# Block 0's TensorE products in pieces of 32 array columns, and the self weighing over 128 rows

## What is computed

```python
def _L0_xcond_ref(x, noise_emb, context, src_mask, ctx_mask, ...):
    NL, D, H, DFF = (6, 128, 16, 512)
    HD = D // H
    ...
    for i in range(NL):
        xn = _adaln(x, noise_emb, n1_w[i], n1_b[i])
        qkv = xn @ qkv_w[i].T
        q, k, v = jnp.split(qkv, 3, axis=-1)
        ...                                # rope on q and k
        a = _attn(q, k, v, src_mask).reshape(B, L, D) @ so_w[i].T
        x = x + a
        xn = _adaln(x, noise_emb, n2_w[i], n2_b[i])
        q = _rope((xn @ cq_w[i].T).reshape(B, L, H, HD))
        k = _rope((context @ ck_w[i].T).reshape(B, LC, H, HD))
        v = (context @ cv_w[i].T).reshape(B, LC, H, HD)
        a = _attn(q, k, v, ctx_mask).reshape(B, L, D) @ co_w[i].T
        x = x + a
        xn = _adaln(x, noise_emb, n3_w[i], n3_b[i])
        h = jax.nn.gelu(xn @ f1_w[i].T + f1_b[i], approximate=False)
        x = x + (h @ f2_w[i].T + f2_b[i])
    return x
```

## Time and profile before

| | |
|---|---|
| median of 3 runs | 6555.9 us (6546.36 to 6572.31) |
| the profiled execution's own time | 6555.0 us |
| its span, first to last instruction | 6553.2 us |
| mean granted TensorE clock | 0.953 of full speed |
| block 0, first weighing's transposes to last | 224.8 to 3390 us of the span |
| matmuls (and as many weight loads) in the span | 56229 |

### The profile page before, as it was taken

How to read it: one execution, slowest core, us unless ns; L and a number is a source line. 1 busy time by engine, 2 the same in 40 slices (tenths; PEclk the granted TensorE clock), 3 DMA queues, 4 the chain that set the end, 5 groups by cost and what they waited for, 6 DMA issues and landing times.

```text
span 6553.2 us, 141305 instructions
## 1 busy us (share of the span) xinstructions
PE 6048.2 (92%) x56229; PEld 4426.8 (68%) x56229; DVE 3934.0 (60%) x8724; ACT 3319.4 (51%) x6401; POOL 2241.2 (34%) x2180
## 2 busy tenths in 40 slices
PE   5899899998999989999989999999789999989998
PEld 4666576665766657666653777777557777756983
DVE  3777777777777777777765334444544444444553
ACT  1565666656566565666653334444333333333763
POOL 4555555555555555555520000000001111146440
PEclk8899999999999999999989899999889999999998
DMA  2665656756566565675750010000100000021000
GB/s 58 103 112 86 102 95 100 107 94 105 92 101 110 91 102 96 102 110 90 112 97 1 18 37 31 29 29 29 26 15 10 15 15 11 15 86 33 1 2 22
DMA packets 396488, 407.90 MB, mean 62 GB/s; under 512 B 125575, under 2 KB 372946, under 8 KB 393786
## 3 DMA queue, kind: packets, MB, share of 16 engines
q1 hardware_dynamic: 395834, 398.85, 34.4%
HBM read 158.00 MB, written 0.46 MB: 24 GB/s over the span
## 4 chain that ended last, share of the span: by engine, by line
PE 69%; DVE 9%; POOL 8%; issue 6%; ACT 4%; DMA 2%; POOLq 1%; SPq 1%; DVEq 0%; ACTq 0%
PE psum L2224 10%; PE psum L2191 9%; PE psum L1554 6%; PE psum L1542 6%; PE psum L1528 6%; PE psum L2235 4%; PE psum L1568 4%; PE psum L1576 3%; POOL slot_context L3410 3%; PE psum L1674 2%; DVE row_max L1898 2%; PE psum L434 2%; PE psum L420 2%; PE psum L1683 1%; POOLq L3417 1%
## 5 line engine op out<-in xcount | busy, mean ns | idle before, releaser
L1898 DVE TENSOR_REDUCE row_max<-psum 112x1 f32<-112x500 f32 x2304 | 1442.0, 668 | 274.1 <-PE psum L1542 269.4
L2019 ACT ACTIVATE weights<-psum 125x448 f32<-125x448 f32 x2304 | 1152.5, 544 | 734.0 <-PE psum L1528 718.6
L1528 PEld LDWEIGHTS psum<-query_stack,key_stack 121*125 121x125 bf16 x9216 | 838.4, 140 | 360.9 <-issue 163.9
L1542 PE MATMUL psum<-key_stack,query_stack 97*112 97x500 bf16 x2304 | 904.8, 393 | 103.3 <-DVE row_max L1898 80.3
L1528 PE MATMUL psum<-query_stack,key_stack 121*125 121x112 bf16 x9216 | 921.2, 223 | 72.8 <-ACT weights L2019 65.0
L2775 POOL TENSOR_TENSOR l_ctx_v<-l_ctx_v,l_ctx_w 125x512 f32<-125x512 f32 x48 | 60.8, 1268 | 2186.2 <-DVE l_ctx_v L2769 2186.2
L2224 PE MATMUL psum<-l_ctx_v,l_turned 125*128 125x128 f32 x5376 | 713.7, 281 | 15.9 <-ACT l_turned L2260 12.2
L2302 DVE TENSOR_REDUCE l_stat<-psum 128x1 f32<-128x1500 f32 (+1 forms) x224 | 391.6, 1748 | 543.6 <-PE psum L2191 543.6
L2224 PEld LDWEIGHTS psum<-l_ctx_v,l_turned 125*128 125x128 f32 x5376 | 643.1, 191 | 49.4 <-ACT l_turned L2260 39.7
L1554 PE MATMUL psum<-weights,values 125*17 125x112 f32 x18432 | 674.9, 265 | 0.2 <-ACT weights L2019 0.2
L1554 PEld LDWEIGHTS psum<-weights,values 125*17 125x17 f32 x18432 | 378.0, 97 | 260.6 <-ACT weights L2019 138.7
(11 more groups left out here) (537 smaller groups left out, 10262.5 us busy)
## 6 DMA issues: line engine op xcount, KB each, us to landing
key_stack<-key_parts SPq DMA_DIRECT2D x1728, 125.0 KB, 4.5
ctx_t<-in_ctxT SPq DMA_DIRECT2D x96, 750.0 KB
l_ctx_v<-in_ctxV SPq DMA_DIRECT2D x32, 750.0 KB
query_stack<-query_parts SPq DMA_DIRECT2D x576, 28.0 KB, 3.6
l_ctx_t<-in_ctxT SPq DMA_DIRECT2D x16, 750.0 KB
slot_context<-in_ctxV SPq DMA_DIRECT2D x16, 750.0 KB
key_stack<-ctx_mask_rows SPq DMA_DIRECT2D x576, 3.9 KB
sm_w<-in_sm_w SPq DMA_DIRECT2D x3, 2048.0 KB
```

The lines of the kernel that those rows point to most:

```text
L1528: mm = e.matmul(self.k.psum[0:KN, h, (p % 4) * QC:(p % 4 + 1) * QC], ks[:, p, kt * KN:(kt + 1) * KN], q[:, p * QC:(p + 1) * QC])
L1542: e.matmul(self.k.psum[0:QC, 2 + n % 2, 0:500], q[0:ROWS_MAX, p * QC:(p + 1) * QC], ks[0:ROWS_MAX, p, c * 500:(c + 1) * 500]).then_inc(sel ...
L1898: e.tensor_reduce(self.largest[:, i % PAIRS, i // PAIRS:i // PAIRS + 1], k.psum[0:QC, 2 + i % 2, 0:500], AX.X, ALU.max, negate=True).then_ ...
L2019: e.activation(half(self.p[kt % 2], h), self.k.psum[0:KN, h, 0:HALF], ACT.Exp).then_inc(self.exped.sem, 1)
```

## The change

A helper, `quarters`, does a product in pieces of up to 32 stationary columns, each to its own 32 output partitions, with the same moving operand. All the products of block 0 that had a wider stationary operand go through it: scores, maxima, keys, values, projections, norms, MLP, self scores and their mask. The weighings had 17 columns already. The transposes of fp32 data (1584, 1591, 1683, 1703, 1710) stay whole. The bf16 transpose takes only the 25 columns that are used. The self weighing now runs over 128 rows: `self_pt` and `self_v` have 128 partitions, the rows of `self_v` past the 56 tokens are zero, and the copies into `self_pt` take all partitions.

```diff
+def quarters(e, out, lhsT, rhs, **kw):
+
+    m = lhsT.shape[1]
+    for lo in range(0, m, 32):
+        hi = min(lo + 32, m)
+        mm = e.matmul(out[lo:hi], lhsT[:, lo:hi], rhs, **kw)
+    return mm
...
-            self.spt = [sb(f"self_pt{i}", [S, H * S])[:, :] for i in range(2)]
-            self.sv = sb("self_v", [S, BH, PAIRS, 17])
+            self.spt = [sb(f"self_pt{i}", [128, H * S])[:, :] for i in range(2)]
+            self.sv = sb("self_v", [128, BH, PAIRS, 17])
...
-            mm = e.matmul(self.k.psum[0:KN, h, (p % 4) * QC:(p % 4 + 1) * QC], ks[:, p, kt * KN:(kt + 1) * KN],
+            mm = quarters(e, self.k.psum[0:KN, h, (p % 4) * QC:(p % 4 + 1) * QC], ks[:, p, kt * KN:(kt + 1) * KN],
                           q[:, p * QC:(p + 1) * QC])
...
-        e.matmul(self.k.psum[0:QC, 2 + n % 2, 0:500], q[0:ROWS_MAX, p * QC:(p + 1) * QC],
+        quarters(e, self.k.psum[0:QC, 2 + n % 2, 0:500], q[0:ROWS_MAX, p * QC:(p + 1) * QC],
                  ks[0:ROWS_MAX, p, c * 500:(c + 1) * 500]).then_inc(self.max_scored.sem, 1)
...
-            e.transpose(side.bank(*key)[:, 0:QC // 2].bitcast(BF16), self.m_part,
+            e.transpose(side.bank(*key)[0:1 + 3 * PAIRS, 0:QC // 2].bitcast(BF16), self.m_part[:, 0:1 + 3 * PAIRS],
                         k.ident_b[0:QC, 0:QC]).then_inc(side.filled, 1)
...
                 for r in range(R):
-                    mm = e.matmul(bk[:, r * S:(r + 1) * S], self.qd[:, i % 2, r * 128:(r + 1) * 128],
+                    mm = quarters(e, bk[:, r * S:(r + 1) * S], self.qd[:, i % 2, r * 128:(r + 1) * 128],
                                   of_batch(self.k_rot, b), start=False, stop=True, skip_group_check=True)
...
-                e.tensor_copy(self.spt[i % 2][:, BANK:T], side.bank(*key)[0:S, 0:T - BANK]).then_inc(side.emptied(*key), 1)
+                e.tensor_copy(self.spt[i % 2][:, BANK:T], side.bank(*key)[:, 0:T - BANK]).then_inc(side.emptied(*key), 1)
...
+        e.memset(self.sv[:, :, :, :], 0.0)
```

More of the change, by code:

```diff
@@ L1599, in fixed_tensor @@
             e.wait_ge(side.emptied(*key), side.before(*key))
-            e.matmul(side.bank(*key)[:, 0:QC], self.co, self.att).then_inc(side.filled, 1)
+            quarters(e, side.bank(*key)[:, 0:QC], self.co, self.att).then_inc(side.filled, 1)
         if 0 <= s + 1 < NS and kt == 10:
@@ L1620, in phase_tensor @@
                 e.wait_ge(side.emptied(*key), side.before(*key))
-                e.matmul(side.bank(*key)[:, 0:HALF], k.mean_w, half(k.z, c)).then_inc(side.filled, 1)
+                quarters(e, side.bank(*key)[:, 0:HALF], k.mean_w, half(k.z, c)).then_inc(side.filled, 1)
             if t == at + 2:
@@ L1632, in phase_tensor @@
             e.wait_ge(side.emptied(*key), side.before(*key))
-            e.matmul(side.bank(*key)[:, 0:HALF], self.wm[:, f, :], half(k.xn, c)).then_inc(side.filled, 1)
+            quarters(e, side.bank(*key)[:, 0:HALF], self.wm[:, f, :], half(k.xn, c)).then_inc(side.filled, 1)
         if mlp is not None and t == T_DOWN:
@@ L1639, in phase_tensor @@
             for f in range(4):
-                mm = e.matmul(side.bank(*key)[:, 0:HALF], self.wm[:, 4 + f, :], self.hidden(f), start=f == 0, stop=f == 3)
+                mm = quarters(e, side.bank(*key)[:, 0:HALF], self.wm[:, 4 + f, :], self.hidden(f), start=f == 0, stop=f == 3)
             mm.then_inc(side.filled, 1)
@@ L1649, in phase_tensor @@
             e.wait_ge(side.emptied(*key), side.before(*key))
-            e.matmul(side.bank(*key)[:, 0:HALF], self.wa[:, (0, 1, 4)[n], :], half(k.xn, c)).then_inc(side.filled, 1)
+            quarters(e, side.bank(*key)[:, 0:HALF], self.wa[:, (0, 1, 4)[n], :], half(k.xn, c)).then_inc(side.filled, 1)
         if t - T_SV in range(2):
@@ L1715, in phase_tensor @@
                 e.wait_ge(side.emptied(*key), side.before(*key))
-                e.matmul(side.bank(*key)[:, 0:QC], self.wa[:, 3, :], self.satt).then_inc(side.filled, 1)
+                quarters(e, side.bank(*key)[:, 0:QC], self.wa[:, 3, :], self.satt).then_inc(side.filled, 1)
     def tensor(self, e):
@@ L1877, in vector @@
         e.memset(self.m_part[:, 0:1], 1.0)
-        e.memset(self.sv[:, :, :, 0:1], 1.0)
+        e.memset(self.sv[0:S, :, :, 0:1], 1.0)
         e.memset(k.psum[:, 5, :], 0.0)
```

14 lines of the change are left out of this document (7 added, 7 removed).

## The result

| | before | after |
|---|---|---|
| time, us (median, lowest to highest, runs) | 6555.1 (6546.4 to 6572.3, 4) | 6700.1 (6685.4 to 6706.7, 4) |
| span of the profiled execution, us | 6553.2 | 6697.6 |
| block 0, first transposes to last, us | 225 to 3391 | 211 to 3534 |

The ratio is 1.0209, with a 95% interval of 1.0184 to 1.0234: the change costs 2.1%, 145 us. The forecast was 6310 us, with a range up to 6542. Block 0 takes 157 us more (3323 against 3166) and starts 14 us earlier; what comes behind it takes the same time in both. So the loss is where the change is.

The account below looks back on a forecast made before the run. TensorE's order of work was taken to set the pace in block 0. Savings of 225 + 65 + 77 = 367 us, two thirds kept (245), took 6555 to 6310 us; whole range 6188 to 6542, the forecast's own 6190 to 6430.

Parts of the forecast that it names:

- Step 1: Block 0, changes of TensorE's tiling shape: 833 fewer pairs at 0.27 us each, 225 us saved.
- Step 2: Score products in block 0: with overlapping loads each of 9216 takes 50 ns, 7 less, 65 us saved.
- Step 3: Self scores in block 0: 14 passes of 107 ns take 50 ns each in pieces, 77 us saved.
- Step 4: Maxima, keys, values, MLP, projections: stream longer than load, so four pieces abreast cost what one whole product does, 0.
- B: Scores and maxima: bf16 pieces don't stream four abreast at full rate; about 7050 us at factor 2, chance 0.08.
- C: The 2304 score halves: each start takes 25 ns whatever its length; 6735 us, chance 0.07.
- D: Weight loads of the score pieces: they go one after another, costing 212 us; 6542 us, chance 0.08.
- Step 5: Issue of 49500 more pairs of matmul and load, nearly all in block 0: taken as 0, bound 92 us.
- Rival E: Block 0: TensorE's instructions arrive too late, some tens of us up to some hundreds; chance 0.04 on the slow side.
- Step 6: The rest: no wait added, self weighing's copies as long as before, one memset more; no cost in us given.
- what is late next: Block 0's slots: VectorE and chains through other engines limit the gain; two thirds of 367 us kept, 245 us.
- rival A: Block 0: VectorE and the DMA queues take most of the saving; with a third kept 6433 us, chance 0.13.

Follow-up runs that it names:

- light transfers: Changed kernel with block 0's key copies cut to 50 of 500 columns and context transfers to 125 columns in later slots, engines' work the same: 6401.9 us.

## Why the prediction was wrong

**Step 1, shape changes: right.** The losses of 0.10 on entering and 0.12 on leaving are gone where pieces stand on either side, and stay where a transpose follows (0.50 us). 0.27 for a pair fits the sums above. Around the value products it was a little more: the weighing and the values behind it took 1.48 us before (1508.67 to 1510.15) and take 1.26 now, which with the 0.10 in front of the weighing is 0.32, and undoing it there cost 0.29.

**Step 2, scores: right.** 16 pieces in 0.20 us are 50 ns a product. **Step 3, self scores: right.** 56 pieces take 0.69 us where 14 x 50 ns = 0.70 was worked out, so 0.81 us are saved of 1.50. The version with whole self scores lost 32 us in spite of 43 us of waits won. That the self weighing now runs over 128 rows was not tried by itself.

**Step 4: right for the stream.** A maximum in four pieces takes 0.21 us, as one whole product did, so bf16 pieces stream four abreast and rivals B, C (20 starts within 0.41 us, where 25 ns each would make 0.50, and 16 within 0.20) and D are out. But "cost 0" holds for the stream alone: these products were cut for a shape change that was not worth their instructions. With the value products alone made whole the kernel was 118 us faster (one run).

**Step 5, issue: wrong, and this is the step that failed.** It asked how fast TensorE starts instructions that have arrived, found 12 in 90 ns, and took 0 with 92 us as the bound. TensorE starts them fast indeed. What it did not ask is how fast they arrive. The page of before had the row (450 fetches of 16 KB on the instruction queue), and from it and the earlier trace rows one could work out some 250 matmuls and loads a fetch and about 10 us a block in block 0, and about 4.3 us a block after, at the time that was forecast (2920 us for 676 blocks). What no row of before shows is the price of a fetch that is late, since there it almost never is (9 waits, 4 us). Rival E named this (2.1 times as many instructions per us), put it at "some tens of us up to some hundreds", and gave it a chance of 0.04. The waits came to 394 us more, where the step had 0. A cost with no row that bounds it and a factor of two on its cause deserved far more than that, and the range should have reached to the other side of before.

**Step 6 and what is late next: right in kind, with luck in the figure.** Two thirds of 367 us kept is 245, and 394 us of waits less the 145 measured are 249. That the two agree to 4 us is luck: the second takes each us of wait for one us lost and leaves out the clock, which the prediction left at its old level and which can have cost up to 58 us. The step also counted four light slots in a period, where the trace of before has two of 26.3 us. With light transfers the light slots take 25.8 us in the median against 24.7 worked out, with some waits left in them. TensorE's waits for the maxima grew from 75 to 119 us, so VectorE takes back a part, as step 6 and rival A have it; how much of the third that was not kept is VectorE's was not measured. VectorE did not come to 90% of the light slot shown: it was busy for 21.0 of 25.1 us.

## What to carry to other kernels

Before cutting products into more pieces, divide TensorE's instructions by the fetches of the instruction queue and see how long one block will last: here the supply was often late when a block of 256 was run in less than some 4 to 5 us. Then cut only the products that gain from it (a load longer than the stream, a shape change on a path that TensorE sets); the best version here cuts the scores and maxima next to a weighing and the self scores, leaves the rest, and is 1.6% faster than before with half again as many shape changes as the slower, fully cut one.

## What the runs showed of the chip that I had not expected

- TensorE's instructions come in blocks of 256 (16 KB). In all kernels here, with about 300 to 730 blocks in block 0, waits of over 0.3 us without a releaser come at each 256th instruction and nowhere else in block 0; the kernels with about 300 blocks have none.
- A late block costs up to 3.9 us, on average 1.3 in the changed kernel (counted from 0.3 on). In that kernel the fetch itself takes 1.4 us in the mean of all blocks, and 1.7 in the median where TensorE stood, which is about a third of the 4.9 us from entry to entry. The other two thirds are 1.7 us from the entry to the fetch and 1.5 us from its end to the next entry.
- Other transfers set the pace of the supply: 4.9 us a block at a DMA share of 0.56, 4.0 us at 0.13. Taking away the large context transfers did nearly nothing (381 us of waits against 398), taking the small key copies as well nearly everything (91).
- bf16 pieces on four groups of columns stream at full rate, 112 columns 16 times in 0.20 us, with their loads hidden.
- Idle time of TensorE came with time at the lower clock: the granted clock was 0.98 before, 0.96 in the changed kernel and 0.94 in it with half of the maxima. It takes no wait at a 256th instruction for that: before with half of the maxima has 0.96 too.

Two things stay open. Where TensorE stood, there are 1.4 to 1.6 us in the median of each kernel with many such waits between the end of a fetch and the first instruction of its block (in the example 1.29), and 1.3 to 1.9 between the entry and the fetch; nothing in the traces says what fills them. And why the key copies delay the supply so much more than the context transfers is not shown. The number of packets is the same in all these kernels, and bytes alone don't tell: 66 MB less of context took 17 us of waits away, 193 MB less of keys 290.
